# A four-stage layer kernel: the normalised input turned by VectorE and carried by DMA, a z block and a few other steps moved

## The chip, the cores and the metric

The kernel runs on one core of a Trainium2 chip. The metric is the device time of one execution in microseconds (us). Three executions of the kernel before took 3183.87, 3190.09 and 3195.75 us; the median is 3190.09 us. All tensors are float32, apart from a small bf16 mask and a few operands marked float32r.

## What is computed

The input x has 4 batches of 1024 tokens of 512 numbers. Four stages follow one another, each with a residual: mixer A, a feed-forward stage F, mixer B, and F again with the same weights.

```python
x = x + attn_a(layernorm(x))      # state-space mixer, 16 heads of 64, state 64
x = x + ffn(layernorm(x))
x = x + attn_b(layernorm(x))      # state-space mixer, 64 heads of 16, state 128
x = x + ffn(layernorm(x))

# a mixer (B; A differs in widths and in where z enters the norm)
proj = x @ in_proj_w                              # columns: z (1024), xBC, dt
xBC  = silu(causal_conv4(xBC) + conv_b)
dt   = softplus(dt + dt_bias);  dA = exp(-dt * exp(A_log))
state = state * dA + (dt * x) (outer) B ;  y = C . state + D * x     # a scan over tokens
out  = rmsnorm(y) * norm_w * silu(z)
return out @ out_proj_w
```

The change leaves stage F's work alone; it touches mixers A and B and the loads at the head of the program.

## The kernel before, in words

**Tiling.** A mixer walks over 16 steps ("supertiles") of 256 tokens; one step holds two tiles j = 0, 1 of 128 tokens. Within step i the scan of tokens of step i is computed in two halves, and between its parts the projections of step n = i + 1 are computed as filling. Steps 0, 14 and 15 are written out, steps 1 to 13 are a loop. Step 0 has no predecessor whose last tile must be finished (`prev` is false), step 15 has no successor (`nxt` is false); so 14 steps of each mixer have both.

**The order on TensorE** is a hand-written list of names (`head` and `schedule`, in `mixer_phase`): `zza`, `zzb` are the last two 128-column blocks of z of the present step; `xT0..3` transpose the convolved x; `BG` (or `BT`, `GT`) is B transposed and B times C; `seg` builds the exponents of a decay slot, `ydiag` uses the slot; `yoff` is C times the state; `prs`, `prt`, `pout` are the sum of squares, the turned sum and the output projection of the previous tile (`rs0`, `rt0`, `out0` those of tile 0); `xnT0`, `xnT1` transpose the normalised input of the next step; `small` and `sums` are cumulative sums; `dt`, `blk0..`, `z0a`, `z0b`, `z1`, `z2` are projections of the next step; `state0`, `state1` are the state updates; `ident0`, `ident1` add y1 into the bank of y.

**Two work banks.** All of these but `seg`, `ydiag` and `ident` write into one of two PSUM banks in turn (`is_use`, `Section.bank`). A use may start only when the one two places before it has been read out (`freed`). So an engine that is late with a copy holds up TensorE two uses later. `use` issues the matmuls, after the wait for their own inputs.

**The input of a step.** SyncE (SP) loads 256 tokens into `x_in` (`load_x`, which waits for `xn_ready`). VectorE (DVE) takes statistics (`norm_stats`), GpSimd (POOL) the root, and DVE writes the normalised `xn` (`norm_apply`), in the second half of step n - 2. In the head of step n - 1 TensorE transposes `xn` in eight 128x128 blocks (`xnT0`, `xnT1`), and ScalarE (ACT) copies the two banks into `xnT` (`xnT_copy`). All projections of the step multiply `w_in` with `xnT`. `zza` and `zzb` of step i still read the `xnT` of step i, so they stand before the transposes.

**The order on the other engines** is that of the code in each `supertile`. DVE in the head: `masked_gt` (gt), `square_sums` (copies the bank of `prs`), `from_state` (two y1 products that free the banks of `yoff0a`, `yoff0b`), `rms_var`, `make_xdt(0)`, `slot_mult`, `out_scale`, `slot_mult`, `make_xdt(1)`, `out_add` (frees the bank of `pout`), `small_sums`. ACT in the head: copies of zza, xT and BT, `square` of the previous tile, copy of zzb, `gate_silu` (needs all of z), `slot_exp`. POOL: skip, y1 + skip, xw, state decay. SP: `load_x`, then per step the stores and residual loads, each waiting for `out_done` or for a store.

**The start.** Constants are built first, in a block of their own that ends for all engines together; in it ACT loads the vectors of stage F (12 transfers of 512 numbers). Then mixer A: SP loads x, w_in in two parts, w_out and 16 pieces of a mask (SBUF to SBUF, 32 KB each); ACT loads six small vectors of the mixer, of which three have 1024 to 1152 elements of 4 or 16 bytes. DVE waits for all six (`small_loaded`), and ACT's `xnT_copy` of the start stands behind what DVE then prepares. After the prologue (projections of step 0) DVE scales w_out by norm_w in 8 instructions (`w_out_ready`), and TensorE waits for that before step 0. Mixer B starts in the same way.

## Time and profile before

One execution was profiled. Its own device time is 3185.51 us, its span (first to last instruction) 3183.8 us; 1.7 us lie around the span. It stands 4.6 us under the median of the three timed runs.

| what | value |
|---|---|
| timed runs, median | 3190.09 us |
| profiled execution, own time | 3185.51 us |
| its span | 3183.8 us |
| TensorE busy | 2839.6 us, 89% |
| VectorE busy | 2071.5 us, 65% |
| ScalarE busy | 1248.4 us, 39% |
| GpSimd busy | 975.0 us, 31% |
| mean granted TensorE clock | 0.953 of full speed |

Stage A lies from about 10 to 1210 us, the first F to 1460 us, B to 2900 us, the second F to the end. A busy time is the sum over an engine's instructions; "idle before <-X" in a row is the time for which the engine stood still ahead of that instruction, and the instruction X whose end released it. The rows on which the prediction rests have a section of their own below.

### The profile page before, as it was taken

To read this page: it belongs to the slowest core of one execution; us is meant where nothing else is said; L and a number is where in the kernel's file an instruction comes from. 1 tells how busy PE (TensorE), PEld (TensorE's weight loads), DVE (VectorE), ACT (ScalarE), POOL (GpSimd) and SP (SyncE) were. 2 spreads that over 40 slices of the span, in tenths; PEclk is the share of its full clock that TensorE was granted. 3 is DMA by queue.
4 is the path that set the end of the run, shared out by engine and by line. 5 is a ranking of instruction groups with operands and counts; after the bars stand their busy time and mean duration, and the time that the engine had idled before them with its cause. 6 is when DMAs were issued, how large, how long until landed. Compare 5 with 4: busy or idle time off the path is not lost. (4 is left out here: it accounts for less than half of the span.)

```text
span 3183.8 us, 54365 instructions
## 1 busy us (share of the span) xinstructions
PE 2839.6 (89%) x19824; PEld 1872.3 (59%) x19824; DVE 2071.5 (65%) x3697; ACT 1248.4 (39%) x2098; POOL 975.0 (31%) x618
## 2 busy tenths in 40 slices
PE   4999999999999996993899999999999999997896
PEld 4666666666666663453666666666666666664453
DVE  3565665665566562485777777877777777776267
ACT  2433434334443331331444444444444444443232
POOL 1232222332233230251233332333233333223135
PEclk9999999999999998996899999999999999998898
DMA  3000000000000005144000000000000000000533
GB/s 117 14 20 26 20 20 20 20 26 26 20 20 20 20 14 225 52 147 158 11 21 20 20 13 20 20 20 10 16 20 20 20 20 13 13 15 29 217 104 134
DMA packets 80673, 140.16 MB, mean 44 GB/s; under 512 B 18120, under 2 KB 18632, under 8 KB 79568
## 3 DMA queue, kind: packets, MB, share of 16 engines
q1 hardware_dynamic: 60048, 126.29, 11.2%
q10 hardware_dynamic: 20544, 12.79, 1.5%
q8 instruction: 51, 0.84, 0.1%
q14 instruction: 30, 0.25, 0.0%
HBM read 104.98 MB, written 33.55 MB: 44 GB/s over the span
## 5 line engine op out<-in xcount | busy, mean ns | idle before, releaser
L525 PE MATMUL work<-b_xnT,b_w_in 128*128 128x256 f32 x2304 | 564.6, 397 | 39.9 <-DVE b_state L1096 29.2
L525 PE MATMUL work<-a_xnT,a_w_in 128*128 128x256 f32 x2176 | 505.0, 388 | 10.0 <-DVE a_w_out L1227 5.8
L525 PEld LDWEIGHTS work<-b_xnT,b_w_in 128*128 128x128 f32 x2304 | 434.5, 195 | 127.8 <-DVE b_state L1096 36.0
L525 PEld LDWEIGHTS work<-a_xnT,a_w_in 128*128 128x128 f32 x2176 | 411.6, 193 | 83.1 <-issue 18.1
L1081 DVE TENSOR_TENSOR b_decay<-b_decay,b_gt 128x1024 f32<-128x1024 f32 x256 | 340.1, 1366 | 27.4 <-ACT b_decay L799 23.4
L799 ACT ACTIVATE b_decay<-seg 128x1024 f32<-128x1024 f32 x256 | 251.6, 1022 | 201.6 <-PE seg L649 200.9
L960 DVE SCALAR_TENSOR_TENSOR b_cv<-b_pre,b_conv_w,b_cv 128x256 f32<-128x256 f32 x480 | 249.6, 548 | 58.8 <-ACT b_cv L745 50.9
L1286 POOL TENSOR_TENSOR a_y<-a_y,a_skip 128x1024 f32<-128x1024 f32 x32 | 106.5, 3327 | 548.2 <-DVE a_y L1070 548.2
L1251 POOL TENSOR_TENSOR rhs<-b_l_side,of_head 128x1024 fp32r<-128x1024 f32 x32 | 83.2, 2600 | 609.3 <-DVE b_l_side L1050 609.3
L630 PE MATMUL work<-a_w_out,a_yz 128*128 128x512 f32 x512 | 248.8, 642 | 21.8 <-ACT a_xnT L729 18.1
L630 PE MATMUL work<-b_w_out,b_yz 128*128 128x512 f32 x512 | 230.8, 604 | 23.7 <-ACT b_xnT L729 15.6
L960 DVE SCALAR_TENSOR_TENSOR a_cv<-a_pre,a_conv_w,a_cv 128x256 f32<-128x256 f32 x432 | 189.7, 482 | 66.5 <-ACT a_cv L745 60.8
L630 PEld LDWEIGHTS work<-a_w_out,a_yz 128*128 128x128 f32 x512 | 102.5, 206 | 146.5 <-issue 119.9
L630 PEld LDWEIGHTS work<-b_w_out,b_yz 128*128 128x128 f32 x512 | 95.6, 192 | 137.2 <-issue 108.8
L1286 POOL TENSOR_TENSOR b_y<-b_y,b_skip 128x1024 f32<-128x1024 f32 x32 | 97.6, 3051 | 222.6 <-DVE b_y L1070 222.6
L1081 DVE TENSOR_TENSOR a_decay<-a_decay,a_gt 128x1024 f32<-128x1024 f32 x64 | 152.6, 2406 | 8.2 <-ACT a_decay L799 7.7
L751 ACT COPY a_z_raw<-work 128x256 f32<-128x256 f32 (+1 forms) x96 | 42.3, 441 | 283.2 <-PE work L525 283.2
L663 PE MATMUL y<-b_decay,b_xdt 128*32 128x128 f32 x4096 | 140.1, 277 | 3.7 <-DVE b_decay L1081 3.7
L663 PEld LDWEIGHTS y<-b_decay,b_xdt 128*32 128x32 f32 x4096 | 104.3, 110 | 46.6 <-issue 29.9
L1480 PE MATMUL y<-f_x1T,f_gate_w 128*128 128x512 f32 x256 | 126.7, 626 | 1.5 <-ACT f_x1T L1605 1.5
L744 ACT COPY b_pre<-work 128x256 f32<-128x256 f32 x160 | 59.9, 374 | 167.1 <-PE work L525 167.1
L751 ACT COPY b_z_raw<-work 128x256 f32<-128x256 f32 (+1 forms) x96 | 42.6, 444 | 194.4 <-PE work L525 194.4
(309 smaller groups left out, 4733.4 us busy)
## 6 DMA issues: line engine op xcount, KB each, us to landing
f_d_w<-in_L_ffn_d_w SPq DMA_DIRECT2D x4, 4096.0 KB, 24.0
f_x_in<-x_mid ACTq DMA_DIRECT2D x12, 1024.0 KB, 5.9
a_x_in<-in_L_attn_a_x SPq DMA_DIRECT2D x16, 512.0 KB, 3.7
a_x_res<-in_L_attn_a_x SPq DMA_DIRECT2D x32, 256.0 KB, 2.6
x_mid<-a_x_res SPq DMA_DIRECT2D x32, 256.0 KB, 2.0
f_x_res<-x_mid SPq DMA_DIRECT2D x8, 1024.0 KB, 5.5
f_bc_w<-x_mid SPq DMA_DIRECT2D x8, 1024.0 KB, 5.4
b_x_in<-x_mid SPq DMA_DIRECT2D x16, 512.0 KB, 3.6
```

Of the source, the lines that this page charges most:

```text
L525: mm = nc.tensor.matmul(dst, w_in[:, k, col:col + m], xnT[:, k, :], start=(k == 0), stop=(k == KD - 1))
L630: mm = nc.tensor.matmul(bank[:, :], yz[:, k, :], w_out[:, k, :], start=(k == 0), stop=(k == KE - 1))
L663: mm = nc.tensor.matmul(ybank[32 * q:32 * q + 32, slot * P:(slot + 1) * P], xdt[:, j, 4 * slot + q, 16 * odd:16 * odd + 32], decay[:, slot ...
L744: nc.scalar.copy(pre[0:m, b, HALO:], bank[0:m, 0:SUP])
L751: nc.scalar.copy(z_raw[:, got[0]:got[-1] + 1, :], sec.bank(name)[:, 0:len(got) * SUP].rearrange("p (b t) -> p b t", t=SUP)).then_inc(z_rea ...
L799: nc.scalar.activation(decay[:, slot_buffer(j, s)].rearrange("p h l -> p (h l)"), seg[s % 2][:, :], ACT.Exp).then_inc(exp_done, 1)
L960: ins = nc.vector.scalar_tensor_tensor(out=cv[0:m, b, :], in0=pre[0:m, b, t:t + SUP], scalar=conv_w[0:m, b, t:t + 1], in1=cv[0:m, b, :], o ...
L1081: nc.vector.tensor_tensor(d, d, gt[:, j].unsqueeze(1).to_broadcast([P, 8, P]), ALU.mult).then_inc(m_ready, 1)
L1251: nc.gpsimd.tensor_tensor(c["rhs"][1][:], l_side[:, 1].unsqueeze(1).to_broadcast([P, 8, P]), c["of_head"][:].unsqueeze(2).to_broadcast([P, ...
L1286: nc.gpsimd.tensor_tensor(y1[:], y1[:], skip[:], ALU.add).then_inc(y1x_ready, 1)
L1480: mm = nc.tensor.matmul(ybank[:, (m % 2) * 512:(m % 2 + 1) * 512], gate_w[:, k, m * P:(m + 1) * P], x1T[n][:, k, :], start=(k == 0), stop= ...
```

## The change

- The normalised input is written over `x_in`. DVE then transposes it in 32x32 blocks into a new buffer `turned` (one instruction per tile). SP carries it in 16 SBUF-to-SBUF transfers of 32 KB (runs of 128 bytes at the target) into `xnT`. TensorE's `xnT0`, `xnT1` and ACT's two copies are gone. `dt` waits for the 16 transfers; `load_x` waits for `turned_ready`.
- `zzb` stands right behind `zza` on TensorE and ACT; the carry of the next step waits for it, since it overwrites `xnT`.
- `ident0` stands in the head, ahead of `small1`; `state0` stands ahead of the last `ydiag` of tile 0; on DVE `state_add(0)` stands ahead of `gate(0)`, and `make_xdt(0)` and `make_xdt(1)` stand earlier.
- x, w_in and the six small vectors of mixer A are loaded in the block of the constants; the vectors of F and of mixer B are loaded by SP during the start of A. The load of w_out, in B that of the z columns too, and the mask pieces come after the first carry.
- w_out is scaled by norm_w in the head of step 0, and only the first `out0` waits for it.

```diff
+        @block.sync
+        def _(sp):
+            load_in(sp, early["x_in"], early["w_in"], ...)
+            load_z(sp, early["w_in"], w, early["z_loaded"])
         @block.scalar
...
-                for name, dst in c["ffn"].items():
...
+                load_vectors(act, c["vectors"][m.tag], weights[m.tag], m.H, c["vectors_loaded"][m.tag])
...
         def head(prev, nxt):
-            return (["zza", "xT0", "xT1", "xT2", "xT3"] + b_and_g + ["seg0.0", "zzb"]
-                    + (["prs"] if prev else []) + ["yoff0a", "yoff0b"] + (["prt"] if prev else [])
-                    + (["xnT0", "xnT1"] if nxt else []) + (["pout"] if prev else []) + ["small1"])
+            return (["zza", "zzb", "xT0", "xT1", "xT2", "xT3"] + b_and_g + ["seg0.0"]
+                    + (["prs"] if prev else []) + ["yoff0a", "yoff0b"] + (["prt", "pout"] if prev else [])
+                    + ["ident0", "small1"])
...
-                if p == 0:
-                    steps += ["ident0"]
+                if p + 1 == NP:
+                    steps += state_steps(0)
                 steps += [f"ydiag0.{2 * p}", f"ydiag0.{2 * p + 1}"]
-            steps += (["z0a"] if nxt else []) + state_steps(0)
+            steps += ["z0a"] if nxt else []
...
+                def carry(n, sec):
+                    if sec:
+                        sp.wait_ge(work_full, sec.full("zzb"))
+                    sp.wait_ge(turned_ready, FREE + 2 * n + 2)
+                    for q in range(4):
+                        for r in range(4):
+                            sp.dma_start(xnT[32 * q:32 * q + 32].rearrange("p k (j r b) -> p r k j b", j=2, r=4)[:, r],
+                                         turned[32 * r:32 * r + 32, q]).then_inc(xnT_loaded, 16)
...
-                def step(i, m, prev, nxt):
+                def step(sec, i, m, prev, nxt):
                     if m is not None:
                         load_x(m)
+                    if nxt is not None:
+                        carry(nxt, sec)
                     if prev is not None:
                         store(prev, 1)
...
-                        pe.wait_ge(xnT_ready, FREE + 2 * n + 2)
+                    if name == "dt":
+                        pe.wait_ge(xnT_loaded, 256 * (n + 1))
...
                     for j in range(2):
-                        nc.vector.tensor_scalar(xn[:, j, :], x_in[:, j, :], mv[:, j, 0:1], ln_r[:, j:j + 1],
+                        nc.vector.tensor_scalar(x_in[:, j, :], x_in[:, j, :], mv[:, j, 0:1], ln_r[:, j:j + 1],
                                                 ALU.subtract, ALU.mult).then_inc(xn_ready, 1)
+                    for j in range(2):
+                        dve.wait_ge(xn_ready, FREE + 2 * n + j + 1)
+                        nc.vector.transpose(turned[:].rearrange("p q k j b -> p j k q b")[:, j],
+                                            x_in[:, j, :].rearrange("p (k q b) -> p k q b", q=4, b=32)
+                                            ).then_inc(turned_ready, 1)
...
                     masked_gt(sec)
+                    make_xdt(sec, 0)
                     if prev:
                         square_sums(sec, "prs")
                     from_state(sec, 0)
                     if prev:
                         rms_var(sec, "prt")
-                    make_xdt(sec, 0)
+                    make_xdt(sec, 1)
                     slot_mult(sec, 0, 0)
...
                     slot_mult(sec, 0, 1)
-                    make_xdt(sec, 1)
                     if prev:
                         out_add(sec, "pout", i - 1, 1)
+                    else:
+                        norm_into_w_out()
                     small_sums(sec, 1)
...
                             if g + 1 == NS and NP > 1:
+                                state_add(sec, 0)
                                 gate(sec, 0)
```

## Rows read from the trace of the kernel before

**Rows 1.** Busy time by window, one of A, one of B (columns: PE, PEld, DVE, ACT, POOL).
```profile
320.00:400.00 80.00, 76.27 (x447) 54.94 (x447) 52.39 (x106) 32.53 (x63) 21.43 (x12) 1.00 0.06 20
1600.00:1680.00 80.00, 74.31 (x688) 50.87 (x687) 62.96 (x99) 38.85 (x61) 26.88 (x14) 1.00 0.07 21
```

**Rows 2.** Timeline of PE in a step of A (start us, us, what, idle before).
```profile
362.21 1.99 PE L525 MATMUL work<-a_xnT,a_w_in 128*128 128x256 f32 x8
...
368.70 1.99 PE L525 MATMUL work<-a_xnT,a_w_in 128*128 128x256 f32 x8
...
373.87 1.09 PE L549 MATMUL work<-ident,a_xn 128*128 128x128 f32 x8 [0.29 <-DVE a_y L1070]
376.24 7.13 PE L630 MATMUL work<-a_w_out,a_yz 128*128 128x512 f32 x16 [1.28 <-ACT a_xnT L729]
...
384.21 1.96 PE L554 MATMUL work<-a_w_in,a_xnT 128*128 128x16 f32 x16 [0.48 <-DVE a_x_res L1126]
```

**Rows 3.** Timeline of PE in a step of B.
```profile
1622.72 1.99 PE L525 MATMUL work<-b_xnT,b_w_in 128*128 128x256 f32 x8
...
1629.24 1.99 PE L525 MATMUL work<-b_xnT,b_w_in 128*128 128x256 f32 x8
...
1636.78 7.13 PE L630 MATMUL work<-b_w_out,b_yz 128*128 128x512 f32 x16 [1.10 <-ACT b_xnT L729]
...
1645.71 2.00 PE L554 MATMUL work<-b_w_in,b_xnT 128*128 128x64 f32 x16 [1.36 <-DVE b_x_res L1126]
...
1679.71 1.99 PE L525 MATMUL work<-b_xnT,b_w_in 128*128 128x256 f32 x8 [1.95 <-DVE b_state L1096]
```

**Rows 4.** Timeline of ACT in the head of A, of DVE in the head of B.
```profile
368.42 1.15 ACT L810 ACTIVATE a_sq<-a_yz 128x512 f32<-128x512 f32 x2
...
1634.58 3.44 DVE L1009 TENSOR_TENSOR b_xdt<-b_xt,b_dt 128x512 f32<-128x512 f32 x2
```

**Rows 5.** Timeline of DVE behind the normalisation, in A and in B.
```profile
428.61 0.35 DVE L1040 TENSOR_SCALAR a_hi<-work,sign_row 128x128 fp32r<-128x128 f32 x1 [3.03 <-PE work L592]
...
1702.45 2.36 DVE L1081 TENSOR_TENSOR b_decay<-b_decay,b_gt 128x1024 f32<-128x1024 f32 x2 [1.13 <-ACT b_decay L799]
```

**Rows 6.** Transfers by line: issue in ns min/median/max, then time to landing.
```profile
L133 ACTq DMA_DIRECT2D in_beta<-in_L_ffn_in_beta x1: 520/520/520, 1.3 to 1.3; - x1
...
DMA to landing us min/median/max: 2.2/2.4/2.4
...
L483 SPq DMA_DIRECT2D masks<-masked_bf x16: 590/591/10640, 12.8 to 32.4; - x16
...
DMA to landing us min/median/max: 4.2/6.8/19.8
```

**Rows 7.** Timelines of ACT's queue, DVE and PE at the two starts.
```profile
14.89 12.27 ACTq L880 DMA_DIRECT2D a_norm_w<-in_L_attn_a_norm_w  x1
...
14.21 0.69 DVE L920 BATCH_NORM_STATS2 a_stats<-a_x_in 128x6 f32<-128x512 f32 x1 [4.86 <-DMA a_x_in<-in_L_attn_a_x]
...
16.82 1.00 DVE L931 TENSOR_SCALAR a_xn<-a_x_in,a_mv,a_ln_r 128x512 f32<-128x512 f32 x2 [0.84 <-POOL a_ln_r L1257]
...
35.72 0.17 DVE L1201 TENSOR_SCALAR a_a_low<-a_a_log 128x16 f32<-128x16 f32 x1 [17.58 <-DMA a_norm_w<-in_L_attn_a_norm_w]
...
37.77 3.57 PE L554 MATMUL work<-a_w_in,a_xnT 128*128 128x16 f32 x16 [14.06 <-ACT a_xnT L729]
...
1468.24 1.00 DVE L931 TENSOR_SCALAR b_xn<-b_x_in,b_mv,b_ln_r 128x512 f32<-128x512 f32 x2 [0.81 <-POOL b_ln_r L1257]
...
1491.70 3.65 PE L554 MATMUL work<-b_w_in,b_xnT 128*128 128x64 f32 x16 [13.45 <-ACT b_xnT L729]
```

**Rows 8.** Timeline of PE at the first step of A and of B.
```profile
75.74 3.78 PE L525 MATMUL work<-a_xnT,a_w_in 128*128 128x256 f32 x8 [5.78 <-DVE a_w_out L1227]
...
98.89 11.43 PE L525 MATMUL work<-a_xnT,a_w_in 128*128 128x256 f32 x44 [2.90 <-DVE a_parts L1041]
...
1533.97 3.78 PE L525 MATMUL work<-b_xnT,b_w_in 128*128 128x256 f32 x8 [8.01 <-DVE b_w_out L1227]
```

More of the change, by code:

```diff
@@ L125, in build_constants @@
     c["ffn_loaded"], c["ffn_count"] = ctx.enter_context(nc.semaphore("ffn_loaded")), 16 * 12
+    c["ffn_w"] = ffn_w
+    c["weights"] = weights
+    c["vectors"] = {m.tag: vectors(sb, m) for m in mixers}
+    c["vectors_loaded"] = {m.tag: ctx.enter_context(nc.semaphore(f"vectors_loaded_{m.tag}")) for m in mixers}
     made, built = (ctx.enter_context(nc.semaphore(n)) for n in ("const_made", "const_built"))
+    early = c["early"] = first_mixer_buffers()
+    c["masked_bf"] = early["masked_bf"]
     with nc.Block() as block:
+        @block.sync
+        def _(sp):
+            w = weights[mixers[0].tag]
+            load_in(sp, early["x_in"], early["w_in"], early["xs_src"], w, early["x_loaded"], early["xbc_loaded"])
+            load_z(sp, early["w_in"], w, early["z_loaded"])
         @block.scalar
@@ L379, in is_use @@
             return not step.startswith(("seg", "ydiag", "ident"))
-        pro_steps = ["xnT0", "xnT1", "dt"] + blocks + ["z0a", "z0b", "z1", "z2", "sums", "small0"]
+        pro_steps = ["dt"] + blocks + ["z0a", "z0b", "z1", "z2", "sums", "small0"]
         epi_steps = ["prs", "prt", "pout"]
@@ L506, in step @@
                         load_res(nxt, 0)
+                carry(0, None)
+                if not early:
+                    load_z(sp, w_in, w, z_loaded)
+                sp.dma_start(w_out[:], w["out_proj"].rearrange("(k p) n -> p k n", p=P)).then_inc(out_loaded, 16)
                 load_x(1)
                 load_res(0, 0)
+                if later:
+                    for b in range(4):
+                        for q in range(4):
+                            sp.dma_start(c["masks"][32 * q:32 * q + 32, b], c["masked_bf"][32 * b:32 * b + 32]
+                                         ).then_inc(c["masks_loaded"], 16)
+                    with nc.allow_non_contiguous_dma(reason="small vectors"):
+                        load_ffn_vectors(sp, c["ffn"], c["ffn_w"], c["ffn_loaded"])
+                        load_vectors(sp, c["vectors"][later.tag], c["weights"][later.tag], later.H,
+                                     c["vectors_loaded"][later.tag])
                 before.clear(sp)
-                step(0, 2, None, 1)
+                step(first(), 0, 2, None, 1)
                 with sp.Fori(0, NSUP - 3) as r:
-                    step(r + 1, r + 3, r, r + 2)
-                step(NSUP - 2, None, NSUP - 3, NSUP - 1)
-                step(NSUP - 1, None, NSUP - 2, None)
+                    step(body(r), r + 1, r + 3, r, r + 2)
+                step(last_but_one(), NSUP - 2, None, NSUP - 3, NSUP - 1)
+                step(last(), NSUP - 1, None, NSUP - 2, None)
                 store(NSUP - 1, 1)
@@ L725, in link @@
                     act.wait_ge(a_chain, steps.next())
-                def xnT_copy(sec, j):
-                    act.wait_ge(work_full, sec.full(f"xnT{j}"))
-                    nc.scalar.copy(xnT[:, :, j * P:(j + 1) * P],
-                                   sec.bank(f"xnT{j}")[:, :].rearrange("p (k t) -> p k t", k=KD)
-                                   ).then_inc(xnT_ready, 1)
                 def softplus(sec):
@@ L1128, in out_add, with norm_into_w_out @@
                                                    ).then_inc(out_done, 1)
+                def norm_into_w_out():
+                    dve.wait_ge(out_loaded, 16)
+                    for k in range(KE):
+                        ins = nc.vector.tensor_scalar(w_out[:, k, :], w_out[:, k, :], norm_w[:, k:k + 1], None, ALU.mult)
+                    ins.then_inc(w_out_ready, 1)
                 def supertile(sec, prev, nxt):
@@ L1224, in _ @@
                 exponent_sides(0)
-                dve.wait_ge(out_loaded, 16)
-                for k in range(KE):
-                    ins = nc.vector.tensor_scalar(w_out[:, k, :], w_out[:, k, :], norm_w[:, k:k + 1], None, ALU.mult)
-                ins.then_inc(w_out_ready, 1)
                 supertile(first(), False, True)
```

136 lines of the change are left out of this document (66 added, 70 removed).

## The prediction

> **What bounds the kernel now.** I read three views in this order: busy time by window, the timelines of one step of each mixer engine by engine, and the timelines of the two starts. The windows show TensorE busy for 76.3 of 80 us in A and 74.3 in B at a granted clock of 1.00, with VectorE at 52 and 63 us and the DMA engines at 6 to 7% [rows 1]. So TensorE sets the pace of both mixers, and what counts is its removed work and its idle gaps. In the timeline of PE the reader is to see two places in the head where it stands still around the transposes: 1.28 us before `pout` in A and 1.10 us in B, both released by ACT's copy of the turned input; then 0.48 us and 1.36 us before `dt`, released by the residual add [rows 2, 3]. B has one more, 1.95 us before `z0b`, released by the state add [rows 3]. At each start TensorE waits 14 us for `dt` (14.06 and 13.45), and before the first step 5.78 and 8.01 us for the scaling of w_out [rows 7, 8].
>
> **The transposes and the copies.** A step with both neighbours loses 1.09 us of transposes (8 matmuls; B's row reads the same and isn't shown) and the wait for the copy, 1.28 us in A and 1.10 us in B [rows 2, 3]. The 0.29 us before the transposes stays: `pout` now waits for the same y1 product. ACT's two copies lie beside TensorE's work and bring nothing else. `ident0` between `pout` and `small1` is moved work, not added: it is eight 128-column transposes like those removed, about 1.05 us, and goes from later in the step to where TensorE waited for the residual add. GpSimd's y1 + skip, which it needs, is released before `pout` starts, and `pout` lasts 7.13 us [rows 2], so I see no wait. With that cover the wait before `dt` goes: 0.48 us in A, 1.36 us in B.
>
> **What the moves in the head add.** Before, `zzb` (1.93 us to the next start) lay between `seg0.0` and `prs` and covered two things. First, `prs` needs ACT's squares. They end at 368.42 + 1.15 = 369.57, 0.87 us after `seg0.0` [rows 2, 4]; that becomes a wait of 0.9 us in A. In B the same reading gives 0.35 us, since `GT` stands behind `BT` there. Second, DVE now makes xdt(0) before it copies the bank of `prs`, and `yoff0b` needs that bank. In A xdt(0) is one product of 1.2 us and is over in time. In B it takes 3.44 us [rows 4]; gt ends 0.1 us before `seg0.0` does, so the copy of the sums ends at about 3.7 us behind `seg0.0`, where TensorE could begin `yoff0b` at 1.9 us: a wait of 1.8 us. So the head gives per step
>
> - A: 1.09 + 1.28 + 0.48 - 0.9 = 1.95 us,
> - B: 1.09 + 1.10 + 1.36 - 0.35 - 1.8 = 1.4 us.
>
> **The state.** `state0` ahead of the last `ydiag` lets DVE add it while TensorE works on `ydiag` and `z0a`, 3 us or more. B's 1.95 us go [rows 3]. What is late next is the bank of `rs0`, which DVE copies after gate(0) and two convolution blocks; by the present lengths that ends within 0.2 us of TensorE's need, so I book 1.95. In A no such wait exists and I book nothing.
>
> **The turn on DVE.** The trace has no transpose on DVE. Its nearest rows are the 128x512 normalisation, 0.5 us each [rows 7], and the 128x512 product of 1.72 us (half of 3.44) [rows 4]: two instructions cost 1.0 to 3.4 us per step. I take 1.3, nearer to the lower, since it has one input. It stands right behind the normalisation, where DVE has 3.03 us of idle time in A, and in B 1.13 us ahead of the next product [rows 5], whose `ydiag` is 4.4 us further off. At 1.3 us it is hidden; at 3.4 us A would lose 0.4 and B about 0.5 us per step, 13 us in all.
>
> **The carry.** Sixteen issues on SP per step. Issues of this size take 0.52 us (512 runs of 4 bytes from HBM) and 0.59 us (mask pieces, SBUF to SBUF, also 32 KB) [rows 6]; the last one then lands 2.4 us later by the first, 4.2 us at best by the second, which stood behind 7 MB of weights. I take 16 x 0.59 + 2.4 = 11.8 us. It starts when `zzb` is full: 362.21 + 3.9 = 366.1 in A, and `dt` then comes at 384.21 - 1.95 + 1.05 = 383.3, so there are 17.2 us; in B 1626.6 to 1645.4, 18.8 us. The carry is hidden with 5 to 7 us to spare. On SP the store of the previous tile stands behind it, but its own release comes at the residual add just before `dt`, after the last issue; nobody waits. The load of x stands ahead of the carry and is needed only in the second half.
>
> A rule of the Trainium skill speaks against this: the page "DMA: Bandwidth & Descriptors", section "Rules for kernel authors", says to coalesce many small transfers, since below 64 KB one pays mostly overhead. The 12 vectors of F show how far it binds: issued every 0.55 us, each landed 2.2 to 2.4 us later and the later ones no later than the first [rows 6], so the overhead overlaps. What it would mean if it did not overlap is a rival below.
>
> **The starts.** In A `dt` begins at 37.77, behind DVE's wait for norm_w, which landed at 35.7 [rows 7]. Now these vectors are issued from 0.8 us, beside 4.9 MB instead of 7.4. But ACT's last issue blocks: it took 12.27 us and ended at 27.16, 16.7 us after ACT's first [rows 7]; so the block of the constants, which used to end near 9.4, now ends at about 16 to 17. From there: statistics and normalisation 3.6 us (14.21 to 17.82), turn 1.3, carry 11.8: `dt` at about 33.5, a gain of 4.3 us; bounds 0 (the issue blocks 4 us longer) and 9 us (it doesn't block). In B the vectors are long there: normalised at 1469.2 [rows 7], turned at 1470.6, carried at 1482.5 against 1491.70: 9.1 us; bounds 3 us (the carry waits behind w_in) and 12.
>
> **w_out.** The waits of 5.78 and 8.01 us go. The first matmuls after them took 3.78 us where 1.99 is the rule [rows 2, 8], the clock having fallen in the gap: 1.8 us more each. The scaling (3.3 us) now lies in DVE's head of step 0, where TensorE already waited 2.90 us for DVE before `blk0` [rows 8]. xdt and the exponent start earlier by about as much as the scaling takes, which leaves 0.5 us against the change in A and nothing in B. Together 5.78 + 8.01 + 3.6 - 0.5 = 16.9 us.
>
> **The sum.** A head 14 x 1.95 = 27.3; B head 14 x 1.4 = 19.6; B state 15 x 1.95 = 29.3 (step 0 has it too); starts 4.3 + 9.1 = 13.4; w_out 16.9; the two last steps, which had no transposes but get the new waits, about -3. That is 103.5 us. Against the profiled execution's own 3185.5 us it gives 3082; that execution lay 4.6 us under the median of the runs, so I say 3087 us for a median.
>
> **Rivals.**
> (1) The DVE order eats more: xdt(0) in the head runs beside GpSimd and takes longer, the turn costs 3.4 us, and the start of A gives nothing. Then A keeps about 1.0 us per step and B 0.5 + 1.7: 14 + 31 us, with 17 + 7 from w_out and the starts, less 3: 66 us, 3124. For it: in B each DVE product in the head is as long as its slack. Against it: DVE has 17 us of idle time in 80 in B [rows 1].
> (2) Slower: the carry comes late. The price is 15 times what it exceeds the windows of 17.2 and 18.8 us in each mixer; it decides from 0.93 us per issue in A. The mask pieces, with the first one blocked for 10.64 us, took (10.64 + 15 x 0.59)/16 = 1.22 us each [rows 6]; at that rate the carry takes 21.9 us, 4.7 and 3.1 us late: 15 x 7.8 = 117 us, and 3087 + 117 = 3204. For it: 4096 runs of 128 bytes are more pieces than any transfer of the loop has now. Against it: the vectors of F had 512 runs per transfer, twice as many, at 0.52 us, and the DMA engines are 93% idle.
> (3) The small transfers do not overlap: each costs its 2.4 us in turn, 38 us, 21 and 20 us late: about 600 us more, 3700. This is what the rule on coalescing would give at its hardest. The overlap of F's vectors speaks against it.
> (4) The change does not do what it says: TensorE's new waits equal the old ones, and only 15 us or less are left: 3175 to 3190.
>
> **How the numbers follow.** Forecast 0.68, (1) 0.18, (2) 0.08, (3) 0.02, (4) 0.04. The forecast's own spread: starts -10 to +8, turn up to 13 worse, the B wait of 1.8 us between 0 and 3 (plus or minus 22): 3058 to 3125. The range goes from there up over (1) to 3155, leaving out (2), (3), most of (4) and tails. What can be told from no change is 0.5%, 16 us. Faster 0.87, same 0.03, slower 0.10.
>
> **What would show it.** Per step of A and B the period between two `zza` falls by about 2 and 3.3 us. Before `pout` no wait for ACT; before `prs` 0.9 us on ACT's square in A; before `yoff0b` about 1.8 us on the copy of the sums in B; no wait on the state add before `z0b`. `dt` without a wait on a DMA; a row "<- DMA xnT" before it would prove (2). The 16 issues near 0.55 us each, landing 2 to 3 us after the last. A turn of 0.5 to 0.8 us each. `dt` at 33 us in A and 21 us after the first load of B. The forecast is wrong if `dt` waits for the carry, or if the heads shrink by less than 1 us.

## The result and the profile after

The kernel after the change takes 3021.56 us (median of 4 runs, 3020.10 to 3022.64) against 3189.41 us of the kernel before in the same rounds (4 runs, 3183.87 to 3195.75): a ratio of 0.9473, 95% interval [0.9455, 0.9491], 168 us faster. The prediction said 3087 us, with a spread from 3058 and a range up to 3155: the sign was right, the gain was 1.6 times what was said, and the time lies below the range. The profiled execution of after has a span of 3018.4 us against 3183.8, 165.4 us less, at a mean granted TensorE clock of 0.965 against 0.953.

I cut both traces at the start of `xT0` of each step and compare the pieces (us gained):

| piece | before | after | gained | predicted |
|---|---|---|---|---|
| start of A to `dt`, F's end to `dt` of B | 37.77 + 48.1 | 33.72 + 38.7 | 13.4 | 13.4 |
| `dt` to step 1, A and B | 111.41 + 132.86 | 109.23 + 125.41 | 9.6 | 18.9 |
| fourteen steps 1 to 14 of A | 1010.2 | 958.2 | 52.0 | 27.3 |
| fourteen steps 1 to 14 of B | 1242.5 | 1149.1 | 93.4 | 46.9 |
| the rest (A's last step with F, B's last step with F) | | | -3.0 | -3.0 |

Both starts are as predicted. The rest agrees too, but by luck in part: by the granted clock (us times 1 minus the clock) A's last step with F lost 5.9 us more in after than in before, and B's last step with F 4.4 us less, though F's work was not changed. The miss is in the steady steps: 145 us where the sum had 74. The same fourteen steps by window, first of before, then of after (columns: window, us, busy PE, PEld, DVE, ACT, POOL, granted clock, DMA share, GB/s):

```profile
149.18:1159.40 1010.22, 958.33 (x5630) 662.74 (x5629) 612.33 (x1211) 396.53 (x728) 299.16 (x167) 0.98 0.07 21
1624.56:2867.03 1242.47, 1157.82 (x10109) 774.73 (x10108) 942.90 (x1449) 568.09 (x910) 410.18 (x196) 0.98 0.05 17
```

```profile
142.95:1101.18 958.23, 920.29 (x5517) 646.06 (x5516) 620.55 (x1236) 380.39 (x700) 283.26 (x167) 0.99 0.12 30
1551.79:2700.88 1149.09, 1122.08 (x9997) 749.97 (x9996) 912.80 (x1475) 553.12 (x882) 406.81 (x196) 1.00 0.10 25
```

A mean clock of 0.98 looks like nothing, but 2% of 2250 us is 45 us. In windows of 2 us before shows 12 stretches below 0.9 in A and 11 in B, each reaching 0.50 to 0.56 in a window; 0.50 is the lower of the two levels (1.2 GHz; 1.00 is 2.4 GHz). I call such a stretch a fall, and count as lost the sum of 2 us times (1 - granted clock): 23.9 us in A and 18.8 in B. After has one in A (5.1 us lost) and none in B. Two of before's falls, by window, and on PE's timeline:

```profile
446.00:448.00 2.00, 1.18 (x2) 0.66 (x3) 1.91 (x1) 1.97 (x5) 2.00 (x2) 0.76 0.00 0
448.00:450.00 2.00, 2.00 (x3) 0.67 (x2) 1.90 (x5) 0.19 (x1) 2.00 (x1) 0.50 0.00 0
...
1768.00:1770.00 2.00, 2.00 (x6) 1.25 (x4) 0.00 (x0) 0.00 (x0) 0.00 (x0) 0.50 0.00 0
```

```profile
446.82 2.75 PE L630 MATMUL work<-a_w_out,a_yz 128*128 128x512 f32 x3 [1.28 <-ACT a_xnT L729]
...
1767.20 2.18 PE L525 MATMUL work<-b_xnT,b_w_in 128*128 128x256 f32 x6 [1.95 <-DVE b_state L1096]
```

The first stands behind the wait of 1.28 us ahead of `pout`, the second behind the 1.95 us ahead of `z0b`, the same waits as in [rows 2, 3]. A step with a fall is about 1.7 us longer (periods between `xT0` of A 70.6 or 72.3, and 75.3 with two falls; of B 87.5 or 89.1). After has 68.2 in A and 82.1 in B in all steps but A's one. [Rows 1] showed windows at 1.00: neither held a fall. The one of A began at 320 us, behind the fall of its step (at 303 us), and went over into a step of 70.6 us without one.

The waits of TensorE over the same steps, B before, then B after (who waited for what: us in total, times, longest):

```profile
PE work L525 <- DVE b_state L1096: 27.3, 14, 2.0
PE work L554 <- DVE b_x_res L1126: 18.8, 14, 1.4
PE work L630 <- ACT b_xnT L729: 15.6, 14, 1.2
PE work L630 <- DVE b_y L1070: 6.7, 14, 0.5
```

```profile
PE work L679 <- DVE b_y L1106: 10.9, 28, 0.5
PE work L669 <- ACT b_sq L852: 3.9, 13, 0.3
```

The three long waits of B are gone, and in their place stand 3.9 us for ACT's square. The predicted 1.8 us ahead of `yoff0b` are not there. With the transposes (14 x 1.09) the sum is 27.3 + 18.8 + 15.6 + 4.5 + 2.2 + (6.7 - 10.9) - 3.9 + 15.3 = 75.6 us (4.5 and 2.2 are waits ahead of the transposes and of `prt`, gone too), and 18.8 us of lost clock make 94.4 against 93.4 found. For A the same gives 29.2 + 18.8 = 48.0 against 52.0, so 0.28 us a step is left. Most of it is `zzb`: from start to next start it took 1.93 us in its old place; behind `zza` it adds 1.73, since the two together take 3.56 us (343.92 to 347.48 in after) and `zza` alone took 1.83.

PE's timeline in after, the heads of A and B (answers to [rows 2, 3]):

```profile
343.92 3.72 PE L577 MATMUL work<-a_xnT,a_w_in 128*128 128x256 f32 x16
...
353.15 0.64 PE L669 MATMUL work<-a_sq,ones 128*32 128x128 f32 x16 [0.94 <-ACT a_sq L852]
...
356.23 7.13 PE L679 MATMUL work<-a_w_out,a_yz 128*128 128x512 f32 x16 [0.21 <-DVE a_y L1106]
363.20 1.04 PE L732 MATMUL y<-ident,a_y 128*128 128x128 f32 x8
...
364.54 1.96 PE L601 MATMUL work<-a_w_in,a_xnT 128*128 128x16 f32 x16
...
1556.86 0.65 PE L669 MATMUL work<-b_sq,ones 128*32 128x128 f32 x16 [0.31 <-ACT b_sq L852]
1557.43 1.98 PE L650 MATMUL work<-b_state,b_bcs 128*128 128x512 f32 x4
...
1560.20 7.13 PE L679 MATMUL work<-b_w_out,b_yz 128*128 128x512 f32 x16 [0.29 <-DVE b_y L1106]
1567.17 1.04 PE L732 MATMUL y<-ident,b_y 128*128 128x128 f32 x8
...
1568.49 1.90 PE L601 MATMUL work<-b_w_in,b_xnT 128*128 128x64 f32 x16
```

`ident0` fills the time in which the residual add runs, and `dt` follows without any wait. Why the 1.8 us never came stands on DVE and POOL in the head of B (answers to [rows 4, 5]; the first row is the turn, in A):

```profile
336.34 1.30 DVE L966 STREAM_TRANSPOSE a_turned<-a_x_in 128x512 f32<-128x512 f32 x2
...
1556.30 1.28 DVE L1045 TENSOR_TENSOR b_xdt<-b_xt,b_dt 128x512 f32<-128x512 f32 x2
...
1560.12 3.44 DVE L1045 TENSOR_TENSOR b_xdt<-b_xt,b_dt 128x512 f32<-128x512 f32 x2
```

```profile
1553.77 1.93 POOL L1321 TENSOR_TENSOR b_skip<-b_xt,b_d_skip 128x1024 f32<-128x1024 f32 x1 [0.82 <-ACT b_xt L822]
1560.30 2.71 POOL L1327 TENSOR_TENSOR b_y<-b_y,b_skip 128x1024 f32<-128x1024 f32 x1 [4.60 <-DVE b_y L1106]
```

The same pair of products costs 1.28 us while POOL is idle and 3.44 us beside POOL's y1 + skip. The row of 3.44 us in [rows 4] was taken beside POOL; the move put xdt(0) into a stretch where POOL is idle. POOL's add ends at 1563.01 and DVE's pair at 1563.56, 0.55 us later; one of these products alone takes 0.68 us, and the second of the pair took 2.84. The Trainium skill, "SBUF — State Buffer", section "SBUF: two separate sides", states that a GpSimd instruction and a DVE instruction with two SBUF inputs take a shared pair of ports in turn, each for its whole length, while the other blocks. The trace agrees: the product that met POOL's add ended only behind it.

The carry, by line, and on SP's timeline (answers to [rows 6]):

```profile
L524 SPq DMA_DIRECT2D a_xnT<-a_turned x256: 594/611/1345, 21.7 to 1043.9; - x128
L524 SPq DMA_DIRECT2D b_xnT<-b_turned x256: 585/611/1614, 1414.5 to 2629.9; - x128
...
DMA to landing us min/median/max: 1.9/2.0/3.2
```

```profile
347.76 10.44 SPq L524 DMA_DIRECT2D a_xnT<-a_turned  x16
```

It is over at about 360.2 in A, 4.3 us before `dt`, and in B at about 1565.4 (issues from 1552.08 for 11.27 us), 3.1 us before `dt`; the prediction had 5 and 7 us to spare. The two starts and A's first step (answers to [rows 7, 8]):

```profile
33.72 3.57 PE L601 MATMUL work<-a_w_in,a_xnT 128*128 128x16 f32 x16 [33.72 <-DMA a_xnT<-a_turned]
...
81.17 1.97 PE L732 MATMUL y<-ident,a_y 128*128 128x128 f32 x8 [4.52 <-POOL a_y L1327]
...
84.96 5.67 DVE L1169 TENSOR_SCALAR a_w_out<-a_w_out,a_norm_w 128x512 f32<-128x512 f32 x8
```

`dt` came at 33.72 (predicted 33.5). But in step 0 no `pout` covers `ident0`, which waits 4.52 us for POOL, the clock falls in that wait (`ident0` takes 1.97 us where 1.04 is the rule), and the scaling of w_out took 5.67 us where it needed 3.3 before: its first two products, which lie beside POOL, took 1.26 and 2.12 us, the other six 0.47 each. `blk0` then waited 4.05 us for DVE. So this piece gave 9.6 us where 18.9 (with B's state wait of step 0) were booked.

### The profile page after: what moved, and what is told of

Read it like the earlier page. It is cut to its first block and busy times, and to the rows that moved or that the text cites. A ratio compares the mean times of both kernels' runs of the same rounds, so it can differ in the third digit from the quotient of the medians.

```text
span 3018.4 us, 54355 instructions
## 1 busy us (share of the span) xinstructions
PE 2756.5 (91%) x19568; PEld 1824.3 (60%) x19568; DVE 2060.1 (68%) x3761; ACT 1212.4 (40%) x2034; POOL 953.5 (32%) x618
## 5 line engine op out<-in xcount | busy, mean ns | idle before, releaser
L577 PE MATMUL work<-b_xnT,b_w_in 128*128 128x256 f32 x2304 | 544.4, 388 | 3.0 <-DVE b_parts L1077 2.9
L577 PE MATMUL work<-a_xnT,a_w_in 128*128 128x256 f32 x2176 | 496.7, 385 | 5.4 <-DVE a_parts L1077 4.0
L577 PEld LDWEIGHTS work<-b_xnT,b_w_in 128*128 128x128 f32 x2304 | 426.9, 191 | 84.4 <-issue 17.2
L577 PEld LDWEIGHTS work<-a_xnT,a_w_in 128*128 128x128 f32 x2176 | 410.4, 191 | 75.1 <-issue 15.3
L1117 DVE TENSOR_TENSOR b_decay<-b_decay,b_gt 128x1024 f32<-128x1024 f32 x256 | 354.2, 1420 | 12.6 <-ACT b_decay L841 8.5
L1292 POOL TENSOR_TENSOR b_rhs<-b_l_side,of_head 128x1024 fp32r<-128x1024 f32 x32 | 82.0, 2562 | 567.0 <-DVE b_l_side L1086 567.0
L996 DVE SCALAR_TENSOR_TENSOR b_cv<-b_pre,b_conv_w,b_cv 128x256 f32<-128x256 f32 x480 | 222.5, 492 | 46.7 <-ACT b_cv L787 38.9
L679 PE MATMUL work<-b_w_out,b_yz 128*128 128x512 f32 x512 | 228.3, 599 | 12.4 <-DVE b_y L1106 12.4
L679 PE MATMUL work<-a_w_out,a_yz 128*128 128x512 f32 x512 | 233.7, 610 | 6.3 <-DVE a_y L1106 6.2
L1521 PE MATMUL y<-f_d_w,f_gate_w 128*128 128x512 f32 x256 | 111.5, 592 | 0.0
```

The lines of the kernel that those rows point to most:

```text
L577: mm = nc.tensor.matmul(dst, w_in[:, k, col:col + m], xnT[:, k, :], start=(k == 0), stop=(k == KD - 1))
L679: mm = nc.tensor.matmul(bank[:, :], yz[:, k, :], w_out[:, k, :], start=(k == 0), stop=(k == KE - 1))
L996: ins = nc.vector.scalar_tensor_tensor(out=cv[0:m, b, :], in0=pre[0:m, b, t:t + SUP], scalar=conv_w[0:m, b, t:t + 1], in1=cv[0:m, b, :], o ...
L1117: nc.vector.tensor_tensor(d, d, gt[:, j].unsqueeze(1).to_broadcast([P, 8, P]), ALU.mult).then_inc(m_ready, 1)
L1292: nc.gpsimd.tensor_tensor(rhs[1][:], l_side[:, 1].unsqueeze(1).to_broadcast([P, 8, P]), c["of_head"][:].unsqueeze(2).to_broadcast([P, 8, P ...
L1521: mm = nc.tensor.matmul(ybank[:, (m % 2) * 512:(m % 2 + 1) * 512], gate_w[:, k, m * P:(m + 1) * P], x1T[n][:, k, :], start=(k == 0), stop= ...
```

## The experiments

Twelve kernels ran. The summary, with clock falls counted as above in the fourteen steps (mean us between two `xT0`). "More than after" and "less than after" below compare medians of different rounds; the intervals stand against the kernel before in the same rounds.

| run | us | against before, 95% interval | A step | falls A | B step | falls B |
|---|---|---|---|---|---|---|
| before | 3189.41 | | 72.16 | 12 | 88.75 | 11 |
| after | 3021.56 | 0.9473 [0.9455, 0.9491] | 68.45 | 1 | 82.08 | 0 |
| state order undone | 3061.28 | 0.9602 [0.9577, 0.9627] | 68.30 | 0 | 85.34 | 14 |
| before + state order | 3170.23 | 0.9936 [0.9916, 0.9957] | 73.14 | 18 | 86.20 | 4 |
| xdt order undone | 3152.35 | 0.9886 [0.9860, 0.9912] | 71.92 | 13 | 87.84 | 14 |
| the same, add ahead of xdt(1) | 3038.86 | 0.9539 [0.9515, 0.9563] | 68.27 | 0 | 83.29 | 3 |
| before + xdt order | 3162.70 | 0.9924 [0.9899, 0.9949] | 72.17 | 12 | 87.68 | 10 |
| before + one filler | 3178.78 | 0.9974 [0.9962, 0.9985] | 71.67 | 9 | 88.75 | 11 |
| before + two fillers | 3217.51 | 1.0076 [1.0050, 1.0102] | 70.58 | 0 | 92.60 | 20 |
| transposes on TensorE | 3069.51 | 0.9627 [0.9602, 0.9653] | 71.52 | 11 | 83.65 | 0 |
| carry in 32 transfers | 3312.92 | 1.0404 [1.0381, 1.0427] | 77.01 | 14 | 92.08 | 14 |
| square first | 3010.93 | 0.9457 [0.9435, 0.9478] | 68.10 | 4 | 81.72 | 0 |
| scaling later | 3014.16 | 0.9473 [0.9447, 0.9499] | 68.44 | 1 | 82.08 | 0 |
| both | 3005.17 | 0.9437 [0.9416, 0.9457] | 68.10 | 4 | 81.72 | 0 |

The falls of a kernel are counted in the one execution that was profiled, and they differ from execution to execution: 41 executions of the kernel before in the rounds of these experiments took 3179.85 to 3197.30 us, at a mean granted clock of 0.956 in the shortest and 0.949 to 0.951 in the ten longest. Two or three falls more or less in one trace therefore say little by themselves.

### The place of the state

```diff
-                if p + 1 == NP:
-                    steps += state_steps(0)
                 steps += [f"ydiag0.{2 * p}", f"ydiag0.{2 * p + 1}"]
-            steps += ["z0a"] if nxt else []
+            steps += (["z0a"] if nxt else []) + state_steps(0)
```

In the changed kernel, with DVE's state add moved back likewise:

> The changed kernel with one part undone: state0 again behind z0a on TensorE, state_add(0) again behind gate(0) on VectorE. Theory G (the falls of TensorE's clock are set off by idle gaps that the change removed; in B by the 1.95 us wait for the state add): undisturbed B steps rise from 82.1 to about 84.0 us, the wait before z0b is back, and stretches at half clock come back in most B steps, about 1.6 us each; A stays at 68.2 us. Sum 15 x 1.95 + 11 x 1.6 = 47 us: about 3068 us. Rival P (the falls came with the transposes and the wait for ACT's copy, not with the state): 15 x 1.95 = 29 us, no stretches at half clock in B: 3051 us.

It took 3061.28 us, 39.7 more than after, between theory G (3068) and rival P (3051); the falls decide for G. Each of B's steps lost 3.3 us, and a fall stood in every one of the fourteen. PE's timeline and windows behind the wait in this run:

```profile
2106.70 3.56 PE L575 MATMUL work<-b_xnT,b_w_in 128*128 128x256 f32 x8 [1.95 <-DVE b_state L1130]
```

```profile
2106.00:2108.00 2.00, 1.30 (x3) 1.13 (x4) 1.24 (x3) 0.00 (x0) 0.00 (x0) 0.62 0.00 0
```

The matmul behind a wait of 1.95 us took 3.56 us where the rule is 1.99. In B's steady steps the edit is worth 1.7 times its wait (3.26 us against 1.95), 45.7 us in fourteen steps. The whole kernel lost less, because in the profiled execution A's steps were 2.0 us and A's last step with the first F 6.2 us shorter than in after, most of it lost clock in F, which the edit does not touch. The same edit put alone into the kernel before:

> The kernel before with one part of the change alone: state0 ahead of the last ydiag of tile 0, state_add(0) ahead of gate(0). Theory G: undisturbed B steps fall from 87.5 to 85.5 us and B's stretches at half clock vanish (11 of 14 steps had one), A keeps its own: 29 + 18 = 47 us less, about 3142 us. Rival P: 29 us less, 3160 us, and B's stretches stay.

3170.23 us: it gained 15.6 us in its rounds. B did about what was expected (35.7 us shorter, 7 falls fewer, 4 left). But A, where no wait was taken away, was 13.7 us slower in the profiled execution: falls went from 12 to 18, and the same wait ahead of `pout` was followed by 10.12 us of `pout` in one step and 7.13 in another. The profiled execution was one of the longer ones (3172.34 us of 3163.74 to 3172.48), but in all six the mean clock was 0.950 to 0.953, no higher than in the kernel before, though B fell less; so the extra loss of clock is not that of one execution. Why A fell more often stays open. PE's timeline of this run, two steps of A:

```profile
457.05 10.12 PE L632 MATMUL work<-a_w_out,a_yz 128*128 128x512 f32 x16 [1.28 <-ACT a_xnT L731]
...
532.16 7.13 PE L632 MATMUL work<-a_w_out,a_yz 128*128 128x512 f32 x16 [1.27 <-ACT a_xnT L731]
```

### The order of xdt

```diff
                     masked_gt(sec)
-                    make_xdt(sec, 0)
                     ...
-                    make_xdt(sec, 1)
+                    make_xdt(sec, 0)
                     slot_mult(sec, 0, 0)
                     ...
                     slot_mult(sec, 0, 1)
+                    make_xdt(sec, 1)
                     if prev:
                         out_add(sec, "pout", i - 1, 1)
```

> The changed kernel with one part undone: make_xdt(0) again behind the y1 products, make_xdt(1) again behind the second slot_mult. Theory C (VectorE's product is slow only while GpSimd works beside it): xdt(0) in B takes 3.4 us again instead of 1.3, since it falls on GpSimd's y1 + skip, and xdt(1) about 3.9; TensorE loses at most the wait for the residual add, 0 to 0.9 us per B step, 3021 to 3034 us. The prediction's view (early xdt costs TensorE 1.8 us per B step): the late place would be faster by 25 us, 2996 us.

Both expected values missed by far: 3152.35 us, 130.8 more than after, nearly four fifths of the whole gain. The waits of its fourteen steps of A and of B, and `dt` in one step of B:

```profile
PE work L601 <- DVE a_x_res L1162: 25.5, 14, 1.8
...
PE work L601 <- DVE b_x_res L1162: 39.4, 14, 2.8
```

```profile
2147.30 3.00 PE L601 MATMUL work<-b_w_in,b_xnT 128*128 128x64 f32 x16 [2.83 <-DVE b_x_res L1162]
...
2151.50 3.65 PE L577 MATMUL work<-b_xnT,b_w_in 128*128 128x256 f32 x8
```

With the transposes and their wait gone and `ident0` put in, TensorE is ready for `dt` some 1.1 us earlier in B (1.09 + 1.10 - 1.05) and 1.3 in A, but the residual add still stood behind xdt(1), which takes 3.90 us at 2142.61 beside POOL. So TensorE waited 2.83 us in B and 1.84 in A, and 27 of 28 steps had a fall: 64.9 us of waits and 61.5 us of lost clock more than after (25.6 + 41.0 against 5.1). To see whether the lateness of the add or xdt's own time is the price, the next kernel keeps xdt late and moves only the add:

```diff
                     if prev:
                         out_add(sec, "pout", i - 1, 1)
+                    make_xdt(sec, 1)
```

> The changed kernel with both xdt products in the old late places, but the residual add moved ahead of xdt(1). With the add behind xdt(1) that order cost 131 us. Theory (the cost is TensorE's wait before dt for the residual add, and the clock falls behind it; the late products themselves cost little): dt without a wait, A near 68.5 and B near 82.5 us a step, 3021 to 3035 us. Rival (the products in their late places cost by themselves, since both run beside GpSimd and push dt's softplus and the slot products): about 1 us a step in A and 3 in B, 3080 us or more.

3038.86 us, just above the expected 3021 to 3035: 113.5 of the 130.8 us came back. A is at 68.27 us a step; B is at 83.29, since TensorE there waits 0.80 us for `b_parts`, which stands behind xdt(1), and three falls came (A has none). The add's place is what counts, and the late products themselves cost 17 us. The new order put alone into the kernel before:

> The kernel before with the new VectorE order alone: xdt(0) ahead of the copy of the sums, xdt(1) ahead of the first slot product. Theory (this order brings the residual add earlier and so takes away TensorE's wait before dt, 0.48 us in A and 1.36 us in B): 14 x 0.48 + 14 x 1.36 = 26 us, 3159 us. Rival (it only matters once the transposes and the copy no longer hold dt back; here the products move and nothing else): 3180 to 3190 us.

3162.70 us, 24.6 less in its rounds, near the expected 3159, but not by the expected way. In A nothing changed (72.17 against 72.16 us a step, and `dt` still waits 0.47), because there the add waits for `pout` itself and not for DVE. In B the wait fell from 1.36 to 0.40, and the fourteen steps became 15.0 us shorter; the other 10 us lie outside the steady steps, 3.4 of them in A's last step with the first F:

```profile
386.41 1.96 PE L554 MATMUL work<-a_w_in,a_xnT 128*128 128x16 f32 x16 [0.47 <-DVE a_x_res L1126]
...
1637.35 2.00 PE L554 MATMUL work<-b_w_in,b_xnT 128*128 128x64 f32 x16 [0.40 <-DVE b_x_res L1126]
```

What is left, 0.4 to 0.5 us, is the add's own time behind `pout`; only `ident0` between `pout` and `dt` covers it. One and the same edit is worth 25 us before the rest of the change and 131 us behind it.

### Clock falls: work added to shorten them

In the kernel before TensorE is given needless work in the gap ahead of `pout`, which leaves 0.40 us of A's wait of 1.28:

```diff
+    for b in range(KE):
+        nc.tensor.matmul(ybank[:, b * P:(b + 1) * P], ident[:], ident[:],
+                         start=(b % 4 == 0), stop=False, is_transpose=True, ...)
```

> The kernel before with work added and nothing removed: between the transposes of the normalised input and pout, TensorE turns the identity matrix eight times (8 x 128 columns, about 1.05 us) into the y bank, which ident0 overwrites later. It lies in the gap of 1.28 us in A and 1.10 us in B in which TensorE waited for ACT's copy. Theory (the head gap is what sets off A's clock falls): the 12 falls of A's 14 steps go, A's mean step comes down from 72.2 to the undisturbed 70.6 us, 22 us in all; B keeps its falls, which stand behind the state wait: 3163 us. Rival (the gap has no part in the clock): the added work is hidden, or costs up to 0.1 us a step: 3184 to 3188 us.

3178.78 us, 8.5 less, where 22 (theory) or 0 (rival) were expected: the theory holds by less than half. The gain is small but clear of the scatter: ten executions took 3176.03 to 3181.91 us at a clock of 0.955 to 0.958, fourteen of the kernel before in the same rounds 3181.12 to 3196.75. A's falls went from 12 to 9, its lost clock from 23.9 to 15.4 us, and its fourteen steps are 6.9 us shorter; the periods of 75.3 us are gone. In the step looked at, the lower clock now began behind the next gap, the 0.48 us ahead of `dt`. So that gap was filled too, with 4 x 128 columns:

> The kernel before with the filler of 8 x 128 columns ahead of pout, and a second filler of 4 x 128 columns (about 0.5 us) into the same bank between small1 and dt, where TensorE waited 0.48 us in A and 1.36 us in B for the residual add. With the first filler alone 9 of 12 falls of A were left, and the one looked at began behind dt. Theory (it is the idle time of the head as a whole that makes the clock fall, and the gaps that are left decide): A's falls go, 70.6 us a step, 15 us less than with one filler: 3164 us. Rival (the falls move on to the next small gap, of 0.2 to 0.4 us, and stay at about 9, or have nothing to do with gaps): 3176 to 3182 us.

In A this came as the theory said: 70.58 us a step in all fourteen, no fall, 1.1 us a step less than with one filler (15.2 us), at a granted clock of 1.00:

```profile
150.45:1138.63 988.18, 955.21 (x5797) 671.43 (x5796) 612.29 (x1211) 396.53 (x728) 299.29 (x167) 1.00 0.07 21
1602.59:2899.03 1296.44, 1200.27 (x10278) 808.05 (x10277) 944.80 (x1449) 568.77 (x910) 410.15 (x196) 0.96 0.05 17
```

```profile
381.86 0.66 PE L695 MATMUL y<-ident 128*128 128x128 f32 x4
382.41 1.96 PE L555 MATMUL work<-a_w_in,a_xnT 128*128 128x16 f32 x16
```

B, however, became 54 us slower, and the whole kernel took 3217.51 us, 32 more than before in its rounds. The cause is of another kind (last section). For A the two runs show what the 0.02 of mean clock in before's steps were: falls set off by idle time of 0.5 to 1.3 us in the head, worth 22 us together. That the removed transposes make the clock fall by themselves, and not the idle time, does not fit: the fillers are such transposes too, twelve more in a step, and the falls went away with them.

### The turn and the carry

The turn and the carry taken out again, with TensorE's transposes and ACT's copies back in the head, ahead of `pout`; all else as in after:

```diff
-                    nc.vector.transpose(turned[:]..., x_in[:, j, :]...)
-                            sp.dma_start(xnT[32 * q:32 * q + 32]..., turned[32 * r:32 * r + 32, q])
+                        for k in range(KD):
+                            mm = nc.tensor.transpose(bank[:, k * P:(k + 1) * P], xn[:, j, k * P:(k + 1) * P], ident[:])
```

> The changed kernel with its main part undone: TensorE transposes the normalised input between prt and pout again and ACT copies it, no turn on VectorE, no carry; all moves and early loads stay. Per step 1.09 us of transposes and 1.3 (A) or 1.1 us (B) of waiting come back, 28 x 2.3 = 64 us; each start gains about 10 us, since nothing is carried. Theory G: the gap before pout is back in both mixers, so A's stretches at half clock come back (11 x 1.6 = 18 us), perhaps B's too (0 to 18): 3083 to 3101 us. Rival (the clock falls came with the order of the other work, not with this gap): 3065 us, A without stretches at half clock.

3069.51 us, 47.9 more than after and below theory G's 3083 to 3101. A's falls came back as G said, and B's did not; the copy was waited for only 0.60 us in A and 0.42 in B, not 1.3 and 1.1. The turned and carried input is thus worth less than a third of the gain (43.0 us in A's and 22.0 in B's steady steps, less 17.3 that the carry costs at the two starts). In A a step is 3.07 us longer: the transposes and 0.60 us of wait make 1.7, and the falls the rest (11 falls where after has one; a step with one is 71.7 us long, one without 69.95); B pays 1.57 us a step and has no fall. At A's start `dt` came at 23.41 us instead of 33.72, in B 18.2 us behind F's end instead of 25.3. The PE rows of A's head:

```profile
355.80 1.09 PE L590 MATMUL work<-ident,a_xn 128*128 128x128 f32 x8 [0.29 <-DVE a_y L1105]
357.49 8.83 PE L673 MATMUL work<-a_w_out,a_yz 128*128 128x512 f32 x16 [0.60 <-ACT a_xnT L771]
```

How far the carry is from deciding: the same data in twice as many transfers.

```diff
-   sp.dma_start(xnT[32 * q:32 * q + 32]...[:, r], turned[32 * r:32 * r + 32, q])
+   for j in range(2):
+       sp.dma_start(xnT[32 * q:32 * q + 32]...[:, r, j], turned[32 * r:32 * r + 32, q]...[:, j])
```

> The changed kernel with the same bytes carried in 32 transfers of 16 KB instead of 16 of 32 KB. If the issue on SP is what a transfer costs (0.61 us each) and the landing overlaps: 32 x 0.61 + 2.0 = 21.5 us from zzb's end, while dt comes 16.8 us (A) and 16.5 us (B) after it; dt then waits 4.7 and 5.0 us in 15 steps of each mixer, and each start loses 9.8 us: 146 + 20 = 166 us more, about 3187 us, more where the clock falls in the gaps. If the 128-byte runs were what costs, the carry would take 11.8 us as before and the time stay at 3021 us.

3312.92 us, 291 more than after and slower than before. An issue costs the same for 16 KB as for 32 KB, and it lands as soon:

```profile
L525 SPq DMA_DIRECT2D a_xnT<-a_turned x512: 585/601/1503, 22.4 to 1178.1; - x171
...
DMA to landing us min/median/max: 1.8/1.8/3.0
```

```profile
1810.53 3.68 PE L603 MATMUL work<-b_w_in,b_xnT 128*128 128x64 f32 x16 [5.42 <-DMA b_xnT<-b_turned]
```

So the price of the carry is the number of issues times 0.6 us. I expected 3187: the waits came about as worked out (72.4 and 77.1 us in the fourteen steps of A and of B, 5.2 and 5.5 each), but with them each step of B spends about 10 us at the lower clock, and A's 9 (133.1 us lost in the 28 steps, 128 more than after).

### A faster version

Two waits of after point to two edits. ACT's square goes ahead of its copies of zza and zzb:

```diff
+                    if prev:
+                        square(2 * i - 1)
                     z_copy(sec, "zza")
```

> The changed kernel with ACT's square of the previous tile moved ahead of its copy of zza, into an idle stretch of 1.9 us in A and 0.85 us in B. prs then no longer waits for it: 0.93 us per A step and 0.3 us per B step, 15 steps each: 18 us less, about 3003 us. Rival (another wait takes its place: the bank of prs is copied behind VectorE's xdt(0), and yoff0b waits for that): A gains 0.5 us at most, B nothing, 3014 us.

3010.93 us, 10.6 less, between the expected 3003 and the rival's 3014. The wait ahead of `prs` is gone, but 0.47 us now stand ahead of `pout` in A, and A has 4 falls where it had 1; so a step of A gained 0.35 us and not 0.9, one of B 0.36 as the row of 0.31 has it (4.9 and 5.0 us in fourteen steps). The second edit moves the scaling of w_out behind the gate and `ident0` of step 0 behind the first projections:

```diff
-                    else:
-                        norm_into_w_out()
+                                if not prev:
+                                    norm_into_w_out()
```

> The changed kernel with the scaling of w_out moved in step 0 from the head of VectorE to behind gate(0), and ident0 of step 0 behind the dt and first block projections. In step 0 TensorE waited 4.5 us (A) and 3.6 us (B) for GpSimd's y1 + skip and 4.05 and 2.9 us for VectorE, and ran at half clock after that. Expected: 4 to 7 us less per mixer, about 3010 us. If VectorE's small sums are late anyway because of the decay products (5.7 us under GpSimd), only 2 us per mixer: 3017 us.

3014.16 us, 7.4 less, though one of its four executions took 3024.41. The trace bears the gain out: step 0 went from 72.1 to 68.3 us in A and from 86.2 to 83.1 in B, 6.9 together. Both together:

> The two edits of the square and of the scaling together: the sum of both gains, 18 + 11 = 29 us, about 2992 us, if they are independent.

3005.17 us, 16.4 less than after and 179 less than before in the same rounds, the fastest of all. The expected 2992 had the square at its full 0.9 us again.

## Why the prediction was wrong, step by step

- **What bounds the kernel: half right.** TensorE sets the pace. But both windows of [rows 1] and both timelines of [rows 2, 3] held no clock fall; such steps are 70.6 and 87.5 us long, and most steps are 1.7 us longer. The periods of all steps, or one window over a mixer (0.98), would have shown it. I knew the effect and booked it at the starts [rows 8], and put it at nothing in the steps. **This is the first failed step, and the larger:** 18.8 us of lost clock went in A and 18.8 in B, 37.6 together; without this error alone the forecast would have been 3049 us. Undoing the state's move (14 falls back), the undone xdt order and the fillers show that such falls come with the waits and go with them.
- **Transposes and copies: right.** Both are gone, as is their wait, and `ident0` needs none behind `pout`. As said, it covers the add.
- **The new waits in the head: the second failed step.** 0.9 us on the square in A was right (0.94), 0.35 in B too (0.31). The 1.8 us ahead of `yoff0b` in B was wrong: it took xdt(0) at 3.44 us, a row recorded beside POOL; in its new place it takes 1.28 us, and `yoff0b` starts without a wait. B's steps gained 27.7 us more than was booked beside the falls, of which the 1.8 us are 25.
- **The state: right in size** (1.95 us gone, nothing late behind it), but its fall was not counted.
- **The turn: right.** 1.30 us, as taken; that it matched to the digit is luck, since the rows gave only 1.0 to 3.4. **The carry: right.** 0.61 us an issue against 0.59, landing 2.0 against 2.4, and done 4.3 us (A) and 3.1 us (B) ahead of `dt`. Rivals (2) and (3) did not come; 32 transfers show (2) at work, and its price is larger than I gave it, since falls come on top. The rule cited there from the Trainium skill, "DMA: Bandwidth & Descriptors", section "Rules for kernel authors", says that small transfers are mostly overhead. Read as a cost in turn it does not hold here, since sixteen transfers were over 12.4 us after the first issue; it holds in that 16 KB cost the queue as much as 32 KB, 0.60 against 0.61 us.
- **The starts: right** (13.4 of 13.4; 4.05 of 4.3 in A, 9.4 of 9.1 in B). **w_out: too high**, 9.6 of 18.9: `ident0` without cover in step 0, and the scaling beside POOL.
- **The sum.** 103.5 predicted; plus 18.8 + 18.8 for the falls, 27.7 for B's head, 5.9 for A's, less 9.3 for step 0: 165.4. Of the 5.9, some 3 are `zzb`, which is cheaper behind `zza`.
- **The range** reached 29 us below the forecast. It held nothing for falls that go, and for xdt(0) it took 22 us to either side of a row that had been recorded with another neighbour. Added up, its own terms give 3057 to 3132 where 3058 to 3125 is written, and a wait of 0 in place of 1.8 us is worth 25 us, not 22; neither brings the measured time in.

## What to carry to other kernels

Before an engine's gap is priced, compare the periods of all steps, not one step: a gap of 1 to 3 us on TensorE can cost up to its own length again in lower clock (0.7 times with the state's move undone, once with the xdt order undone), and taking it away pays that too. Take a duration on VectorE from a row with the same neighbour on GpSimd as in the new place. An order of small operations that is worth little alone can carry most of a change that takes away the slack which hid it; so try the parts inside the new kernel, not in the old one.

## What the runs showed of the hardware

- **A fall is not tied to one gap.** The same wait of 1.27 us ahead of `pout` was followed by the lower clock in some steps and not in others, and in before with one filler the fall looked at began behind the 0.48 us ahead of `dt`. After's head of A has waits of 0.94, 0.31 and 0.21 us in 4 us and saw one fall in fourteen steps; with 0.94, 0.31, 0.29 and 0.60 it saw eleven.
- **Eight more instructions in a loop can cost tens of microseconds.** The second filler adds four matmuls with their weight loads to each step with both neighbours; the eight matmuls of the first filler had cost nothing of the kind. In B TensorE then stood still up to 4.7 us at a time without any operand or semaphore to wait for, 12 times and 31.0 us in 14 steps, and the queue that carries instructions moved 106 packets, 1.74 MB, in the whole run where the other kernels, that with one filler too, move 51, 0.84 MB. The waits of B, one of them on PE's timeline, and the queue over the whole run and from 1710 to 2700 us, inside B's loop (packets, MB, share of the DMA engines):

```profile
PE work L526 <- issue: 31.0, 12, 4.7
```

```profile
1782.04 2.50 PE L526 MATMUL work<-b_xnT,b_w_in 128*128 128x256 f32 x5 [4.65 <-issue]
```

```profile
q8 instruction: 106, 1.74, 0.2%
...
q8 instruction: 45, 0.74, 0.4%
```

  In the same stretch of time the kernel before, alone or with one filler, has no packet on this queue. The 45 packets come in groups of nine, one group every second step, and three of them lie in or just behind each long stop (1777.8, 1777.9 and 1782.6 us around the stop that ends at 1782.04). So code is loaded anew in every second step of B's loop, and TensorE stands still while that begins. What size of the loop decides it was not tried. The clock fell more often as well (20 falls in B).
- **A short transfer from SBUF to SBUF** of 16 KB or 32 KB in runs of 128 bytes costs 0.60 to 0.61 us of its queue and lands 1.8 to 2.0 us later, also with 16 or 32 of them in a row.
